# Routed experts: gate shares and sums kept in DRAM and fetched as repeated rows, in place of products with a matrix of ones

## The reference, cut to what matters

```
flat = w_dense[:, inv_mapping]                    # tokens x 8 experts x 8
scalar = flat.sum(-1)
soft = softmax(where(flat == 0, -1e9, flat), axis=-1)

def _fused_linear(x, W, qa, qb, scale, w):
    a = einsum('th,krh->tkr', x, qa)              # 64 codes: 8 variants k x rank 8
    b = einsum('tkr,khr->tkh', a, qb)
    return x @ W.T + scale * einsum('tkh,tk->th', b, w)

def expert(..., w):
    xe = x + w @ muW.T
    gate = silu(_fused_linear(xe, gW, ..., w))
    up = _fused_linear(xe, uW, ..., w)
    return _fused_linear(gate * up, dW, ..., w)
y = einsum('fth,tf->th', outs, scalar)
```

## Time and profile before

| | us |
|---|---|
| median of 3 runs | 1020.29 (1018.66 to 1023.12) |
| the profiled execution, own time | 1022.85 |
| its span in the profile | 1020.3 |
| PE busy | 865.2 (85% of the span) |
| DVE busy | 736.0 (72%) |
| ACT busy | 446.2 (44%) |
| mean granted TensorE clock | 0.838 |

### The profile page before, as it was taken

One profiled execution on the slowest core, in us unless ns is written; L12 is line 12 of the kernel. 1 busy time (PEld: TensorE's weight loads), 2 busy tenths in 40 slices (PEclk: granted clock), 3 DMA queues, 4 the chain that ended last, 5 costly groups with the idle time before them and its releaser, 6 DMA issues.

```text
span 1020.3 us, 11627 instructions
## 1 busy us (share of the span) xinstructions
PE 865.2 (85%) x4214; PEld 512.5 (50%) x4214; DVE 736.0 (72%) x974; ACT 446.2 (44%) x679; POOL 166.8 (16%) x251
## 2 busy tenths in 40 slices
PE   5989894489889999989899677788888988779898
PEld 3434662244655555545455344344444657654566
DVE  1776558964557787787678898899994546658777
ACT  2214446642324422221223588789883434622111
POOL 1000000000013532425200162111111000001412
PEclk9899885589979999999899855555558999969999
DMA  8502003100132222240112989987771000000000
GB/s 266 197 3 44 1 0 50 19 2 7 19 48 43 36 35 25 54 59 10 22 25 42 170 150 176 155 146 146 139 145 30 9 1 0 1 1 1 10 11 21
DMA packets 211612, 59.13 MB, mean 58 GB/s; under 512 B 192398, under 2 KB 209892, under 8 KB 211556
## 3 DMA queue, kind: packets, MB, share of 16 engines
q1 hardware_dynamic: 211444, 58.23, 29.5%
q10 hardware_dynamic: 112, 0.17, 0.1%
HBM read 20.62 MB, written 1.05 MB: 21 GB/s over the span
## 4 chain that ended last, share of the span: by engine, by line
PE 52%; DVE 25%; ACT 10%; issue 7%; DMA 4%; POOL 1%; ACTq 1%; DVEq 0%; SPq 0%; POOLq 0%
PE ps L946 48%; ACT xc L1889 5%; DMA arena<-xc 4%; DVE arena L2593 3%; DVE arena L2227 1%; PE ps L1077 1%; DVE arena L2602 1%; PE ps L1389 1%; DVE xc L2399 1%; ACT arena_split L1806 1%; DVE sq L2506 1%; DVE sq L2503 1%; PE ps L472 1%; DVE xn_t L2028 1%; DVE arena L2141 1%
## 5 line engine op out<-in xcount | busy, mean ns | idle before, releaser
L946 PE MATMUL ps<-arena 128*128 128x16 f16 (+7 forms) x1760 | 269.1, 324 | 50.5 <-ACT xc L1889 37.5
L946 PE MATMUL ps<-arena_split 128*128 128x512 f32 (+6 forms) x736 | 199.5, 435 | 18.3 <-DVE arena_split L2405 5.7
L946 PEld LDWEIGHTS ps<-arena 128*128 128x128 f16 (+4 forms) x1760 | 132.4, 130 | 163.1 <-issue 82.5
L946 PEld LDWEIGHTS ps<-arena_split 128*128 128x128 f32 (+6 forms) x736 | 134.4, 196 | 90.3 <-issue 41.0
L1889 ACT ACTIVATE xc<-ps,arena 128x1024 int16<-128x1024 f32 x128 | 153.1, 1201 | 25.8 <-POOL arena L904 13.2
L2593 DVE TENSOR_REDUCE arena<-ps 128x1 f32<-128x1024 f32 x128 | 150.8, 1218 | 13.3 <-PE ps L946 11.0
L946 PE MATMUL ps<-sq,arena 128*64 128x256 f32 (+3 forms) x256 | 80.8, 516 | 8.1 <-DVE sq L2506 8.1
L904 POOL TENSOR_SCALAR arena<-arena 128x1 f32<-128x1 f32 x128 | 34.2, 267 | 182.4 <-DVE arena L2593 182.1
L853 POOL TENSOR_SCALAR arena<-arena 128x512 f32<-128x512 f32 x12 | 23.1, 1924 | 246.8 <-DVE arena L2421 246.8
L1658 ACT ACTIVATE act_buf<-ps 128x512 f32<-128x512 f32 (+2 forms) x34 | 20.3, 597 | 89.4 <-PE ps L946 89.3
L946 PE MATMUL ps<-mean_w,sq 128*128 128x1 f32 x240 | 35.8, 279 | 21.3 <-ACT sq L1623 21.3
(11 more groups left out here) (290 smaller groups left out, 1331.5 us busy)
## 6 DMA issues: line engine op xcount, KB each, us to landing
arena<-in_L_ffn_w SPq DMA_DIRECT2D x4, 640.0 KB, 6.0
arena_split<-arena_split SPq DMA_DIRECT2D x59, 32.0 KB
arena<-xc SPq DMA_TRANSPOSE x96, 3.3
arena<-in_x SPq DMA_DIRECT2D x1, 1024.0 KB, 5.7
arena<-in_ctx SPq DMA_DIRECT2D x1, 1024.0 KB, 8.2
arena<-in_L_xattn_Wkv SPq DMA_DIRECT2D x2, 512.0 KB, 3.9
arena<-in_L_ffn_gate_w SPq DMA_DIRECT2D x1, 1024.0 KB, 10.0
arena<-in_L_ffn_up_w SPq DMA_DIRECT2D x1, 1024.0 KB, 12.5
```

The source lines that it names most:

```text
L946: return pe.matmul(o, l, r, start=start, stop=stop)
```

## The change

PE no longer makes the repeated rows, and ACT no longer copies them. `rep`, `rep_r`, `scalar`, `weight_rows` and `scalar_rows` are gone, with the waits on bank 7 that they brought. Instead DVE copies the gates from PSUM to an fp32 tile `gates`; SP writes each share row eight times to a DRAM tensor (256 KB for expert 0, then 448 rows of 4 KB, 1.8 MB, for the others) and the eight sums to another (32 KB); and for every unit it fetches `wr` (two DMAs of 128 KB) and `sr` (one DMA of 256 KB that repeats one row on 128 partitions). The fetch for unit n + 2 waits for `moe_awd >= n + 1`, the last read of the same half of `wr` by unit n. `load_gates` shrinks from 10 to 6 DMAs. ACT's copy of the gates is cut in two, one for each bank, and alternates with DVE's copies.

```
+            def shares_kept(f0, f1, s):
+                n = (f1 - f0) * NK
+                sp.dma_start(shares_out[f0 * NK:f1 * NK], gates[f0 * NK:f1 * NK].unsqueeze(1).to_broadcast([n, NR, TOK])
+                             ).then_inc(s, 16)
+            def spread(n):
+                f, h = divmod(n, 2)
+                done = load[f"spread{h}"]
+                rows_of = shares_out[f * NK:(f + 1) * NK].rearrange("k r t -> (k r) t")
+                for j in range(2):
+                    sp.dma_start(moe["wr"][64 * j:64 * j + 64, h, :], rows_of[:, tok(h)]).then_inc(done, 16)
+                sp.dma_start(moe["sr"][:, h, :], scalars_out[f, tok(h)].partition_broadcast(P)).then_inc(done, 16)
+            sp.wait_ge(gate_split, 2)
+            shares_kept(0, 1, first_out)
+            sp.dma_start(scalars_out, gates[NE:GATES]).then_inc(first_out, 16)
+            sp.wait_ge(gate_split, 3)
             load_gates(sp, 0, 1)
+            sp.wait_ge(first_out, 32)
+            spread(0)
+            spread(1)
             for part in range(2):
                 load_gates(sp, 1, part)
-            for f in range(2, NF):
+            shares_kept(1, NF, rest_out)
+            sp.wait_ge(rest_out, 16)
+            def next_expert(f):
                 sp.wait_ge(moe_turn_a, 2 * f - 2)
                 sp.wait_ge(moe_turn_d, 2 * f - 2)
                 load_slot(f, f % 2)
-                sp.wait_ge(moe_srm, 2 * f - 2)
+                sp.wait_ge(moe_mu, 2 * f - 2)
                 for part in range(2):
                     load_gates(sp, f, part)
-                if f == 5:
+            next_expert(2)
+            for n in range(2 * NF - 2):
+                sp.wait_ge(moe_awd, n + 1)
+                spread(n + 2)
+                if n % 2 and n < 2 * NF - 5:
+                    next_expert((n + 5) // 2)
+                if n == 9:
                     sp.wait_ge(lx_sum, BATCH)
...
-                mm(ps[:, 7, :], rep_r[64:64 + 2 * NK, :], g[64:64 + 2 * NK], True, True).then_inc(moe_wrm, 1)
-            def scalar(n):
-                f, h = divmod(n, 2)
-                pe.wait_ge(moe_wr, n + 1)
-                mm(ps[:, 7, :], rep_r[96:98, :], gate_rows[96:98, f % 2, tok(h)], True, True).then_inc(moe_srm, 1)
...
-            act.activation(gate_parts[0:GATES, 0, :].rearrange("p (a b) -> p a b", a=2), ps[0:GATES, 6:8, :],
-                           ACT.Copy).then_inc(rt_gates_sb, 1)
-            act.wait_ge(rt_gates_sb, 1)
+            act.activation(gate_parts[0:GATES, 0, 0:HALF], ps[0:GATES, 6, :], ACT.Copy).then_inc(rt_gates_sb, 1)
+            act.wait_ge(gate_split, 1)
+            act.activation(gate_parts[0:GATES, 0, HALF:], ps[0:GATES, 7, :], ACT.Copy).then_inc(rt_gates_sb, 1)
+            act.wait_ge(rt_gates_sb, 2)
             load_gates(act, 0, 0)
...
+            dve.wait_ge(rt_gatest, 1)
+            dve.tensor_copy(gates[:, HALF:], ps[0:GATES, 7, :]).then_inc(gate_split, 1)
             dve.wait_ge(rt_gates_sb, 1)
...
+            dve.tensor_copy(gates[:, 0:HALF], ps[0:GATES, 6, :]).then_inc(gate_split, 1)
+            dve.wait_ge(rt_gates_sb, 2)
+            dve.wait_ge(gate_split, 2)
+            TTN(gate_parts[0:GATES, 1, :], gates, gate_parts[0:GATES, 0, :], ALU.subtract).then_inc(gate_split, 1)
...
             def weighted_codes(n):
                 dve.wait_ge(moe_a, n + 1)
-                dve.wait_ge(moe_wr, n + 1)
+                dve.wait_ge(load[f"spread{n % 2}"], 48 * (n // 2 + 1))
                 TTN(moe["aw"], ps[:, 0, :], moe["wr"][:, n % 2, :], ALU.mult).then_inc(moe_aw, 1)
```

More of the change, by code:

```diff
@@ L176, in build @@
         mu_t = c([D])
-        rep = c([P])
         inv_row = c([NE], I32)
@@ L227, in build @@
                   gmx=c([TT * NF]), gt=c([TT, GATES]))
+        gates = rt["wdT"][0:GATES]
+        shares_out = nc.dram_tensor("gate_shares", (NE, NR, TOK), F32, kind="Internal").ap()
+        scalars_out = nc.dram_tensor("gate_scalars", (NF, TOK), F32, kind="Internal").ap()
         moe = dict(xe=xc[:, 0], s=xc[:, 1], h=sq[:, 0, :], pack=sq[:, 1, :], wr=act_buf[:, :, :], sr=hid_buf[:, :, :],
@@ L307, in build @@
         load = {n: sem("load_" + n) for n in ("ctx", "x", "tid", "l0", "l1", "mu", "moe0", "moe1",
-                                               "l2w", "l2x", "l2", "l3x", "l3", "rows", "gate0", "gate1")}
+                                               "l2w", "l2x", "l2", "l3x", "l3", "rows", "gate0", "gate1", "spread0", "spread1")}
+        first_out, rest_out = sem("first_out"), sem("rest_out")
         turned, evac_act, evac_dve = sem("turned"), sem("evac_act"), sem("evac_dve")
@@ L327, in build @@
         moe_xh, moe_xl, moe_high = sem("moe_xh"), sem("moe_xl"), sem("moe_high")
[L328 to L331, removed]
+        (moe_mu, moe_xe, moe_a, moe_aw, moe_h, moe_s, moe_sm, moe_hg, moe_ad, moe_awd, moe_y, moe_x) = (sem(n) for n in (
+            "moe_mu", "moe_xe", "moe_a", "moe_aw", "moe_h", "moe_s", "moe_sm", "moe_hg", "moe_ad", "moe_awd", "moe_y",
+            "moe_x"))
         pj_ready, pj_used, bias_split = (sem(n) for n in ("pj_ready", "pj_used", "bias_split"))
@@ L585, in load_gates @@
             done, tile = load[f"gate{f % 2}"], gate_rows[:, f % 2, :]
-            for r in ((0, 2 * NK, 32, 32 + 2 * NK, 64), (NK, 32 + NK, 64 + NK))[part]:
+            for r in ((0, 2 * NK, 32, 32 + 2 * NK), (NK, 32 + NK))[part]:
                 row_copy(eng, tile, r, gate_parts[f * NK:(f + 1) * NK, part, :], done)
-            row_copy(eng, tile, 96 + part, gate_parts[NE + f:NE + f + 1, part, :], done)
         def lx_bank(t):
@@ L828, in _ @@
                                     pattern=[[HD, P // HD], [0, HD]], channel_multiplier=-1))
[L830 to L835, removed]
             step(pool.iota(e_col[0:NE, :], pattern=[[0, 1]], base=0, channel_multiplier=1,
@@ L1158, in key_value_sums @@
             def key_value_sums(b):
-                pe.wait_ge(lx_keys, b // 2 + 1)
+                pe.wait_ge(lx_keys, 2 + b)
                 for m in range(KC):
@@ L1184, in _ @@
             pe.wait_ge(moe_ev_dve, 2)
-            pe.wait_ge(rt_gates_sb, 1)
+            pe.wait_ge(rt_gates_sb, 2)
+            pe.wait_ge(gate_split, 2)
             pe.wait_ge(lx_copied, TT)
@@ L1192, in correction @@
                 if h == 0:
-                    pe.wait_ge(load[f"gate{f % 2}"], 160 * (f // 2 + 1))
+                    pe.wait_ge(load[f"gate{f % 2}"], 96 * (f // 2 + 1))
                 if n == 0:
@@ L1305, in unit @@
                 if n == TERN_UNIT:
-                    pe.wait_ge(moe_sr, n + 2)
+                    pe.wait_ge(lx_keys, 2 + BATCH)
                     ternary(2)
@@ L1324, in keys @@
                     pe.wait_ge(bias_split, 1)
-                pe.wait_ge(pj_used, g) if g == 3 else pe.wait_ge(moe_sr, 2 * NF - 2 + g)
+                    pe.wait_ge(tern_part, 3)
+                else:
+                    pe.wait_ge(pj_used, g)
                 projected(0, 2 * g, 7, ctx_t, wkv2)
@@ L1338, in _ @@
             correction(0)
-            scalar(0)
             codes(0)
@@ L1793, in _ @@
                 key_values(t)
-            def weight_rows(n):
-                act.wait_ge(moe_wrm, n + 1)
-                act.activation(moe["wr"][:, n % 2, :], ps[:, 7, :], ACT.Copy).then_inc(moe_wr, 1)
-            def scalar_rows(n):
-                act.wait_ge(moe_srm, n + 1)
-                act.activation(moe["sr"][:, n % 2, :], ps[:, 7, :], ACT.Copy).then_inc(moe_sr, 1)
             def x_high(n):
@@ L2493, in unit @@
                     key_rest(0, 0, k_high, k_rest)
-                dve.wait_ge(moe_sr, n + 1)
+                dve.wait_ge(load[f"spread{h}"], 48 * (f + 1))
                 dve.wait_ge(moe_h, n * 3 + 2)
@@ L2523, in unit @@
                 if n == 2 * NF - 2:
-                    dve.wait_ge(moe_srm, 2 * NF)
+                    dve.wait_ge(moe_mu, 2 * NF)
                     key_scaled(0)
```

24 lines of the change are left out of this document (1 added, 23 removed).

## The result

| | us |
|---|---|
| changed kernel, median of 20 runs | 1025.05 (1019.19 to 1032.3) |
| kernel before, median of 20 runs on the same chips | 1019.91 (1017.13 to 1025.52) |
| ratio | 1.005, 95% interval 1.0033 to 1.0068 |
| profiled execution of the changed kernel: own time, span | 1028.57, 1026.8 |

The change made the kernel 5 us slower, where the prediction had 4 us faster. The page of the kernel after: PE's work is down by 6.4 us and ACT's by 18.5 (446.2 before), and in the chain that ended last DMA has grown from 4% to 7% and SP's queue from 0 to 2%.

What follows compares the result with a forecast made beforehand. The path alternates between PE-then-DVE and PE-only units, so removed products count only in some. Units 3.2 plus start 1.0 gave 4.2 us gained: 1016.1 against the 1020.29 median, range 1011.0 to 1023.6.

Steps and rivals of the forecast that it cites:

- The new DMAs in SP's queue: SP's writes and fetches: a new wait can arise only in unit 1; forecast no wait, with 1.9 us margin.
- the fast end: The 1.8 MB write at 342 GB/s, 5.4 us after 1.7 us landing time; the forecast took this price.
- the slow one: The 1.8 MB write priced from the existing row copies: 127 GB/s with all engines, 14.4 us.
- the start: Before unit 0's codes: fewer ACT issues bring the first correction 0.85 us and codes 1.3 us earlier; 1.0 taken, ends 0 and 1.3.
- SP comes late in unit 1: Rival, 22%: the big write at its slow end makes DVE wait 7.1 us before unit 1's weighted down codes; 1023.2 us.
- point of decision: For the late-SP rival: it decides from a big write of 7.3 us on; at 11.5 us all gain is gone.
- the margin of 1.9: Unit 1: fetched rows land at 308.3 us, DVE wants them past 310, so no wait.
- The units: Products taken from PE: 0.36 + 0.23 us in units 0, 1, 7, 9, 11, and 0.23 in unit 3; 3.2 us.
- The wait for DVE's second gate: Sign in the profile after: PE still waits for it in 11 or more units, 8.1 us plus about 6.
- Copies of ACT: 32 copies of 0.60 us leave ACT, beside PE and DVE: worth nothing, except at the start.
- The clock: Rival, 14%: more PE idle ahead of down codes in units 2, 4, 6, 8; four new clock falls, 6.8 us, 1022.9.
- The product that counts in every unit: Rival, 9%: products removed from PE gain 0.43 + 0.23 us in all 16 units, plus 1.3; 11.9 us, 1008.4.

Runs made afterwards that it cites:

- e7: Changed kernel with each of the two share writes cut into eight, one per copy of a row, so successive packets leave different partitions: 1025.81 us.
- e9: Changed kernel with the first write taken from eight partitions four apart in another tile (expert 0's shares come out wrong): 1022.74 us.
- e1: Changed kernel without the DRAM writes and without the fetches of repeated rows (shares and sums left out of the result): 1016.68 us.
- e2: Changed kernel with SP's two row copies for expert 0 issued ahead of the 256 KB write: 1030.14 us.
- e4: Changed kernel with each share row written once (32 and 224 KB) and repeated eightfold by the fetch that reads it: 1016.37 us.
- e10: Changed kernel with the first write from eight partitions four apart and the second from 112 partitions of another tile (shares wrong): 1018.52 us.
- e8: Changed kernel with rows written once, SP's row copies ahead of the first write, and SP's wait for the second behind the weight loads: 1017.44 us.
- e3: Changed kernel with the 1.8 MB write cut: expert 1's 256 KB first, the rest behind unit 2's fetch, no wait before expert 2's weights: 1024.24 us.
- e5: Changed kernel with SP's row copies ahead of the 256 KB write and the 1.8 MB write cut in two, no wait before expert 2's weights: 1020.06 us.
- e6: Changed kernel with SP's wait for the 1.8 MB write moved behind expert 2's weight loads and row copies: 1023.84 us.

## Why the prediction was wrong

**The step that failed** is the price of the two writes in "The new DMAs in SP's queue". The prediction had the first write landing 2.5 us after SP could start, at the pace of a lone load or store; it took 8.0. It had the big one at 5.4 us behind a landing time of 1.7, so SP held for 7.1, the fast end, because it saw "rows queued one behind another" as in the loads at 9 to 19 us. SP was held for 12.0. By the same count the write cost 10.3, between the fast end and the slow one (14.4, from the row copies' 127 GB/s). What decided was not whether packets are queued (e7) but which partitions they leave (e9). For the first write the nearest row was the row copies, which come from eight neighbouring partitions as well. The window 272.6 to 277 of the kernel before, above, has them: 60 GB/s at a share of 0.49, which is eight engines busy all the time. Read so, the first write of 256 KB costs at least 4.4 us by itself, and more beside the copies. For the big one, from 56 partitions, that trace has no such row; the write moved 210 GB/s.

**What the step left out altogether** is that the first write shares its eight engines with the row copies on the critical path: the DMA share is 0.48 from 273.0 to 280.7 us, no more than one of them alone keeps busy. The prediction let ACT's issues keep 0.93 us each and only asked whether a fetch would be late. They took 1.8 each, and "the start", put at 1.0 us gained, became 3.7 us lost at the first correction. With the write gone, behind the copies or small (e1, e2, e4) the term comes true: the correction is 0.9 us earlier (9.6 to 8.8; predicted 0.85), and unit 0's codes start 12.9 us after the split, 14.3 before: 1.3, the upper end.

**The rival "SP comes late in unit 1"** had the mechanism and the place: a DMA named ahead of DVE's L2410 (now L2406). Its price was 7.1 us by a write of 14.4; with SP held for 12.0 us the wait was 3.5, because the start's own stall had put PE and DVE back too. Where the start was mended (e2) the wait was 10.1. Its point of decision was too mild: in e10 SP was held for 8.0 us, 6.3 by the prediction's count and under its 7.3, and DVE waited 2.0 all the same. SP came to that write 1.0 us later than forecast, the 256 KB fetch landed 3.7 us after its issue and not 3.0, and DVE came about 1 us earlier, so the margin of 1.9 was read too wide as well.

**The units.** Predicted were 5 x 0.59 + 0.23 = 3.2 us. Distances between the sums into `x_t` in e4 against before: unit 1 14.15 for 14.53, unit 7 15.07 for 15.45, unit 9 14.11 for 14.53, unit 11 14.14 for 14.51, unit 3 14.28 for 14.29, and nothing in the even ones at the same clock (units 2, 4, 6, 8: 16.07, 15.56, 16.25, 16.26 in both). So the right units were named, and each gave 0.4 where 0.59 was put; unit 0, from its codes to its sum, gave 0.7. That is 2.3 us in place of 3.2. The wait for DVE's second gate (L2502 in the changed kernel) is in 15 units now and 10.8 us in all: it caps the gain in these units too. The prediction had PE wait about 6 us more for it; it was 2.7. Start and units together give 2.3 + 1.3 = 3.6, the median of e4 3.8 less than before, and the prediction's sum 4.2. The profiled execution of e4 shows only part of it: the start and units 0 to 3 are 2.5 us shorter, but what units 7, 9 and 11 gain is used up by 3.4 us more at half clock between 444 and 500 us.

**Copies of ACT**: 18.5 us less busy. No run has this alone; the start and the units account for all that e1 and e4 gain, so nothing is left for it, as said.

**The clock.** The rival had four new falls, in units 2, 4, 6 and 8, at 1.7 us each. A stretch of 3.4 us at 0.50 does show in unit 4 of the changed kernel, e1, e8 and e10, and not in e2, e3, e4, e5, e6, e7 and e9 nor before. Unit 4 is then 17.1 to 17.2 us long and not 15.6, and unit 5 15.4 and not 15.9: 1.1 us in all. Unit 2 has such a stretch in e1, e3, e6 and e8 (17.2 us and not 16.1), and there it is 1.1 of the 4.1 and 3.9 us that e3 and e6 are above before by the yardstick. So the rival came true in two of its four units at most (e1, e8) and in one in the changed kernel, at two thirds of its price. It is not what makes the changed kernel slow: e1 and e8, with both falls, gain as much as e4, which has none. Their stretch at the start is 3.4 us and not 10.2, so that their half-clock time up to unit 4 is 10.2 in all, as in e4 and before. The half-clock stretches behind the two stalls (17.1 and 6.8 us) are another matter. They go with the stalls: from the start to unit 4 the time at 0.50 is 27.3 us in the changed kernel, 20.5 in e2 and e7, 17 in e3, e6 and e9, 10.2 in e10, 6.8 in e5. Over all executions the mean granted clock was 0.839 in the changed kernel and 0.843 in the one before beside e1 to e4. How much of the stalls' price is waiting and how much is slower work behind it, no run separates.

**The product that counts in every unit**, 1008.4, fell: the kernel without any rows has 1016.68 us.

## What to carry to other kernels

The price of a DMA out of SBUF is read from a transfer with the same source partitions, not from the fastest stream in the trace: here eight neighbouring partitions gave 50 to 60 GB/s, whatever was queued. Write each row once and repeat it in the fetch, which here read DRAM eight times at no cost that showed, and don't write it eight times out of a few partitions. And before a transfer is put in a queue, ask which small transfers on the critical path share its engines; mending one of two stalls can make a kernel slower.

## What had not been expected of the hardware

- A DMA's issue is not a fixed cost. Beside the 256 KB write ACT's four issues took 7.30 us and not 3.2, and beside the 1.8 MB write (e6) SP's five issues took 10.2 us and not 2.6: an instruction that only issues can hold its engine for microseconds. What holds it, the runs don't show; with the write's source spread (e9) the four took 3.97.
- 4 KB packets out of SBUF took 0.61 us from eight neighbouring partitions, 0.30 from 56 partitions and 0.16 from eight partitions four apart or from 112. Rows of DRAM read eight times each (e4) made nobody wait.
- SP's order is worth 10 us of the median here without a byte more or less: e2 and e5 differ only in when and in how many pieces the second write leaves, and in SP's wait for it.
